# Sixty-four-row mask and shift matmuls, turned maxima, and pairwise column maxima in a two-layer transformer kernel

## What is computed

```python
h = _layernorm(x) * (1 + ca) + sa
q, k, v = heads(h @ Wq, 16), heads(h @ Wk, 4), heads(h @ Wv, 4)   # head width 64
q, k = rope(q), rope(k)                    # 4 query heads share one key head
scores = einsum('bkgqd,bkpd->bkgqp', q, k) / 8
scores = where(tril, scores, -1e30)        # query q sees keys 0..q
probs = softmax(scores)
x = x + ga * (einsum('bkgqp,bkpd->bkgqd', probs, v) @ Wo)
```

## Time and profile before

| | |
|---|---|
| median of three runs | 1842.28 us (1834.22 to 1844.19) |
| profiled execution, its own time | 1832.43 us |
| its span, first to last instruction | 1830.6 us |
| TensorE busy | 1629.2 us, 89% |
| VectorE busy | 1075.0 us, 59% |
| ScalarE busy | 703.6 us, 38% |
| mean granted TensorE clock | 0.975 of full; 1.00 in the first attention |

### The profile page before, as it was taken

The page is one execution under the profiler, slowest core; times in us unless marked ns, Lnnn a source line. Parts: engine busy times, 40 slices in busy tenths (PEclk is TensorE's granted clock), DMA queues, the critical chain, the costliest instruction groups (busy, mean ns, idle before and its releaser), DMA issues.

```text
span 1830.6 us, 75756 instructions
## 1 busy us (share of the span) xinstructions
PE 1629.2 (89%) x34444; PEld 1279.7 (70%) x34444; DVE 1075.0 (59%) x2269; ACT 703.6 (38%) x1135; POOL 847.2 (46%) x802
## 2 busy tenths in 40 slices
PE   6899999999999988888987898988989898978993
PEld 4567677777777766677975676766777677767883
DVE  3756666666688865537426566665666665544234
ACT  2334344343434333354542343433334343334341
POOL 2555555555555547437766163423324241016442
PEclk9999999999999999999987999999999999989997
DMA  9800000000000000043344433324141422036666
GB/s 302 262 18 2 8 3 8 2 8 2 8 2 2 8 4 18 15 141 41 91 70 54 86 72 68 81 47 90 43 87 46 89 59 67 15 99 187 202 205 186
DMA packets 103849, 128.05 MB, mean 70 GB/s; under 512 B 11909, under 2 KB 86281, under 8 KB 103064
## 3 DMA queue, kind: packets, MB, share of 16 engines
q1 hardware_dynamic: 82920, 103.39, 20.9%
q0 software_dynamic: 15808, 16.93, 4.9%
q10 hardware_dynamic: 4800, 2.89, 0.6%
HBM read 91.57 MB, written 54.07 MB: 80 GB/s over the span
## 4 chain that ended last, share of the span: by engine, by line
PE 60%; DVE 16%; issue 7%; POOL 6%; DMA 6%; ACT 4%; POOLq 0%; ACTq 0%; SPq 0%; DVEq 0%
PE psum L1182 57%; DVE colmax L1916 3%; DMA arena<-in_pack 3%; ACT prob L1628 2%; DVE colmax L2025 2%; DVE ctx_sum L1928 2%; DMA added_rows<-arena,slot_token 2%; POOL arena L2278 2%; DVE raw L1873 1%; DVE rowmax L1923 1%; POOL added_rows L2290 1%; PE psum L1506 1%; DVE rowmax L2033 1%; ACT arena L1645 1%; PE psum L1249 1%
## 5 line engine op out<-in xcount | busy, mean ns | idle before, releaser
L1182 PE MATMUL psum<-arena 128*32 128x32 f32 (+8 forms) x10296 | 572.6, 251 | 45.9 <-issue 24.3
L1182 PEld LDWEIGHTS psum<-arena 128*32 128x32 f32 (+3 forms) x10296 | 449.1, 126 | 135.8 <-issue 68.2
L1645 ACT ACTIVATE arena<-psum 128x1024 f32<-128x1024 f32 (+1 forms) x192 | 169.3, 882 | 310.0 <-PE psum L1182 309.9
L1182 PE MATMUL psum<-neg_ident,rowmax 128*32 128x128 bf16 (+3 forms) x4352 | 208.6, 249 | 12.9 <-DVE rowmax L2033 8.4
L1182 PE MATMUL psum<-prob,ffw 128*32 128x128 f32 x5120 | 201.5, 275 | 14.8 <-DVE rowmax L1923 13.3
L1916 DVE TENSOR_REDUCE colmax<-psum 128x512 bf16<-128x2048 f32 (+2 forms) x96 | 168.4, 1754 | 77.7 <-PE psum L1182 77.6
L2025 DVE TENSOR_REDUCE colmax<-psum 128x256 bf16<-128x768 f32 (+2 forms) x160 | 178.3, 1115 | 58.0 <-PE psum L1182 55.7
L1660 ACT COPY ctx_sum<-psum 128x384 f32<-128x384 f32 x128 | 61.2, 478 | 384.8 <-PE psum L1182 348.4
L2265 POOL TENSOR_TENSOR arena<-ctx_sum 128x256 f32<-128x256 f32 x128 | 94.2, 736 | 219.5 <-DVE ctx_sum L1928 207.9
L2033 DVE TENSOR_REDUCE rowmax<-psum 128x2 bf16<-128x256 f32 (+1 forms) x192 | 97.9, 510 | 137.2 <-PE psum L1182 136.3
L1182 PEld LDWEIGHTS psum<-neg_ident,rowmax 128*32 128x32 bf16 (+1 forms) x4352 | 135.2, 98 | 50.2 <-issue 30.6
(11 more groups left out here) (242 smaller groups left out, 2454.9 us busy)
## 6 DMA issues: line engine op xcount, KB each, us to landing
arena<-in_pack SPq DMA_DIRECT2D x39, 578.0 KB, 3.8
sent<-in_empty SPq DMA_DIRECT2D x9, 2112.0 KB, 39.9
arena<-qk_parts SPq DMA_DIRECT2D x96, 128.0 KB
q_copies<-arena SPq DMA_DIRECT2D x32, 256.0 KB
prob<-q_copies SPq DMA_DIRECT2D x128, 64.0 KB, 3.6
qk_parts<-arena SPq DMA_DIRECT2D x16, 384.0 KB, 4.9
arena<-sent SPq DMA_DIRECT2D x39, 132.0 KB, 3.2
ffw<-in_L_w SPq DMA_DIRECT2D x16, 256.0 KB, 5.7
```

The lines of the kernel that those rows point to most:

```text
L1182: return pe.matmul(o, lhsT, rhs, start=start, stop=stop, skip_group_check=True)
L1645: act.activation(probs_of(i)[:, :, h0 * P:(h0 + nh) * P], slot(n)[:, 0:(i + 1) * W].rearrange("p (j c) -> p j c", c=W), ACT.Exp, scale=HD1 ...
```

## The change

1. **Shift.** Each matmul used 128 rows and wrote 128 columns for each key block. Now it uses 64 rows (`rows`), half of them for each par: `rowmax` is laid out so that partitions 0 to 63 hold the maxima of par 0 and 64 to 127 those of par 1, with four columns x = (head a, query half). `neg_half` is minus the identity of 64, once on each half of the partitions. There are twice as many matmuls, of half the columns, and par alternates.
2. **Mask.** Four 64-row matmuls of 128 columns instead of two 128-row ones of 256: weights `later_keys` [64 queries, 128 keys] (1e30 where the key is later), `neg_half` streamed.
3. **Maxima.** To lay `rowmax` out so, the turning is done by 16 matmuls with 32 columns of `colmax` as weights, each into its own quarter of the partitions, instead of four with 128.
4. **Column maxima.** VectorE's reduction over j is replaced. ScalarE copies blocks 1 and, for i = 3, 3 to bf16 (`block_copy`); VectorE takes elementwise maxima: one for i = 1, two for i = 2, three for i = 3. The last of i = 3 has all operands in SBUF in bf16.
5. **Setup.** The `causal` constant is three times as large, and VectorE makes `neg_half` and `later_keys`.

```diff
@@ PE, scores
-                        for par in range(2):
-                            ins = mm(scores_of(u)[:, par, i, :], ident_bf[:, :],
-                                     causal[:, :].unsqueeze(1).to_broadcast([P, 2, P]), False)
+                        for half in range(2):
+                            for par in range(2):
+                                rows = slice(HQ * par, HQ * (par + 1))
+                                ins = mm(scores_of(u)[:, par, i, :].rearrange("p (a q) -> p a q", a=2)[
+                                             :, :, HQ * half:HQ * (half + 1)],
+                                         later_keys[rows, half, :],
+                                         neg_half[rows, :].unsqueeze(1).to_broadcast([HQ, 2, HQ]), False)
@@ PE, maxima
-                        for h in range(GRP):
-                            ins = mm(psum[:, CTX, h * P:(h + 1) * P], colmax[:, n % 2, h * P:(h + 1) * P],
-                                     ident_bf[:, :], start=(h == 0))
+                        for x in range(GRP):
+                            a, half = divmod(x, 2)
+                            for quad in range(GRP):
+                                par, low = divmod(quad, 2)
+                                at = (2 * par + a) * P + half * HQ + low * QUAD
+                                ins = mm(psum[QUAD * quad:QUAD * (quad + 1), CTX, x * P:(x + 1) * P],
+                                         colmax[:, n % 2, at:at + QUAD], ident_bf[:, :], start=(x == 0))
@@ PE, shift
-                        for h in range(GRP):
-                            par, a = divmod(h, 2)
+                        for x in range(GRP):
                             for j in range(0, i + 1, 2):
                                 nj = min(2, i + 1 - j)
-                                ins = mm(scores_of(u)[:, par, j:j + nj, a * P:(a + 1) * P],
-                                         rowmax[:, n % 2, h:h + 1].to_broadcast([P, P]),
-                                         neg_ident[:, :].unsqueeze(1).to_broadcast([P, nj, P]), False)
+                                for par in range(2):
+                                    rows = slice(HQ * par, HQ * (par + 1))
+                                    ins = mm(scores_of(u)[:, par, j:j + nj, x * HQ:(x + 1) * HQ],
+                                             rowmax[rows, n % 2, x:x + 1].to_broadcast([HQ, P]),
+                                             neg_half[rows, :].unsqueeze(1).to_broadcast([HQ, nj, HQ]), False)
@@ ACT
+                    elif k == "scores" and s["u"]["i"]:
+                        u = s["u"]
+                        w.wait_ge(scored, u["n"] + 1)
+                        w.wait_ge(colmax_dve, cm_at[u["n"]][1] - 1)
+                        for a, j in enumerate(range(1, u["i"] + 1, 2)):
+                            act.copy(block_copy[:, a, :, :], scores_of(u)[:, :, j, :]).then_inc(block_copied, 1)
@@ DVE, scores
-                            dve.tensor_reduce(colmax[:, n % 2, :].rearrange("p (z c) -> p z c", z=2),
-                                              scores_of(u).rearrange("p z j c -> p z c j"),
-                                              AX.X, ALU.max).then_inc(colmax_dve, 1)
+                            to = colmax[:, n % 2, :].rearrange("p (z c) -> p z c", z=2)
+                            blocks = scores_of(u)
+                            copied += (i + 1) // 2
+                            w.wait_ge(block_copied, copied)
+                            if i == 1:
+                                dve.tensor_tensor(to, blocks[:, :, 0, :], block_copy[:, 0, :, :], ALU.max
+                                                  ).then_inc(colmax_dve, 1)
+                            else:
+                                dve.tensor_tensor(pair_max, blocks[:, :, 0, :], block_copy[:, 0, :, :], ALU.max
+                                                  ).then_inc(paired, 1)
+                                if i == 3:
+                                    dve.tensor_tensor(block_copy[:, 1, :, :], blocks[:, :, 2, :], block_copy[:, 1, :, :],
+                                                      ALU.max).then_inc(paired, 1)
+                                pairs += i - 1
+                                w.wait_ge(paired, pairs)
+                                dve.tensor_tensor(to, block_copy[:, 1, :, :] if i == 3 else blocks[:, :, 2, :], pair_max,
+                                                  ALU.max).then_inc(colmax_dve, 1)
```

More of the change, by code:

```diff
@@ L31 @@
 GRP = 4
+HQ = P // 2
 E, F = 8, 512
@@ L166, in shape_constants @@
         "ident": np.eye(P, dtype=np.float32),
-        "causal": np.where(p[:, None] <= p[None, :], 0.0, NEG).astype(np.float32),
+        "causal": np.stack([np.where(p[:, None] <= p[None, :], 0.0, NEG)] + [
+            np.where(p[:, None] % HQ + HQ * half >= p[None, :], 0.0, -NEG) for half in range(2)], 1).astype(np.float32),
         "first_token": (np.arange(HALF * E)[:, None] // E * S).astype(np.float32),
@@ L235, in build @@
         prob = sb("prob", [P, 2, 4 * BANK])
-        causal_f = prob[:, 0, 0:P]
+        causal_f = prob[:, 0, 0:3 * P].rearrange("p (a c) -> p a c", a=3)
         colmax = sb("colmax", [P, 2, BANK], BF16)
@@ L340, in build @@
         xn1 = ctx_sum[:, 1, 1, :].rearrange("p (n d) -> p n d", n=NT)
+        block_copy = ctx_sum[:, 1, 0, :].bitcast(BF16).rearrange("p (a z c) -> p a z c", a=2, z=2)
+        pair_max = ctx_sum[:, 1, 1, BANK // 2:].bitcast(BF16).rearrange("p (z c) -> p z c", z=2)
+        neg_half = ctx_sum[:, 1, 1, 0:HQ // 2].bitcast(BF16)
+        later_keys = ctx_sum[:, 1, 1, HQ // 2:HQ // 2 + P].bitcast(BF16).rearrange("p (a c) -> p a c", a=2)
         small = raw[:, 1, :]
@@ L1009, in build @@
             semaphore(n) for n in ("x_full", "x_loaded", "moments_ready", "normed", "rot_a", "swapped", "key_rest"))
+        block_copied, paired = semaphore("block_copied"), semaphore("paired")
         scored, colmax_dve, colmax_act, max0_full, max0_done, shifted, prob_ready, ctx_full, ctx_drained, recip = (
@@ L1779, in tile_list @@
                                       ALU.subtract).then_inc(tiles_ready, 1)
+                copied = pairs = 0
                 dve.memset(ones_bf[:, :], 1.0)
@@ L1797, in _ @@
                         dve.tensor_scalar(neg_ident[:, :], ident[:, :], -1.0, None, ALU.mult)
+                        dve.scalar_tensor_tensor(neg_half, ident[:, 0:HQ], -1.0, ident[:, HQ:P], ALU.mult, ALU.subtract)
                     elif k == "mod_first":
@@ L1825, in _ @@
                         w.wait_ge(d_x, XREST)
-                        dve.tensor_copy(causal[:, :], causal_f).then_inc(consts_ready, 1)
+                        dve.tensor_copy(causal[:, :], causal_f[:, 0, :])
+                        dve.tensor_copy(later_keys, causal_f[:, 1:3, :]).then_inc(consts_ready, 1)
                     elif k == "stat":
```

## The result

Over twenty runs of each the changed kernel took 1844.59 us and the kernel before 1837.51 us. The ratio is 1.0039, with a 95% interval of 1.0023 to 1.0056: slower by some 7 us, where 4 us faster were forecast. The profiled execution took 1840.52 us (before 1832.43). Measured twice more beside the kernel before, the changed kernel gave 1.0061 and 1.0062.

The account below looks back on a forecast made before the run. Groups were taken as TensorE-bound mostly, plus VectorE's work between i = 3 scores and values. Groups +0.07, -0.19, -0.34, +0.02 made -0.44 a batch, -3.5 over eight; taken -4: 1828.5 profiled, 1838.5 against the median, range 1823 to 1856.

Parts of the forecast that it names:

- Leg 3: TensorE from the shift of i = 2 to the mask, 4.30 us in the second group: forecast -0.37 us.
- leg 2: From the mask after the i = 3 shift to the values, 3.79 us in the second group: forecast +0.03 us.
- leg 4: From the mask of i = 3 to the values, 4.80 us in the second group: forecast +0.51 us.
- two new changes +0.20: Tile-shape changes added on TensorE, shift to side step and side step to maxima: forecast +0.20 us in leg 1.
- leg 1: TensorE from the shift of i = 3 to the mask, 250.98 to 255.50 in the second group: forecast -0.36 us.
- the fourth group's +0.02: Forecast sum over the fourth group of a batch: leg 1 0, leg 2 -0.12, total +0.02 us.
- 1 to 2 us: Batches 5 and 6, where expert selection loads VectorE: its shorter work may give 1 to 2 us.
- theory 1: Steady groups: TensorE's 64-row shift, mask and turned maxima gain; casts and pairwise maxima lose, above all in leg 4.
- theory 2: Start of batch 0: the loss is made there, costing 7 us, and the steady state hardly moves.
- Rival 2: VectorE's detour in leg 4 decides, slower once it grows more than 0.62 us: about +11, 1853 us; chance 0.20.
- Rival 3: 64-row bf16 pairs don't run at once, +24, 1866 us, chance 0.09; in experiments, tile changes cost TensorE more than saved.
- Rival 1: The gain arrives: leg 4 keeps its 4.80 us, -2.48 a batch, -20 in all, 1822 us; chance 0.16.

Follow-up runs that it names:

- the two half kernels: Kernel before with 64-row shift, mask and turned maxima, reduction kept: 1937.69 us, ratio 0.9941; kernel before with only casts and pairwise maxima: 1968.36 us, 1.0105.
- one-cast run: Changed kernel with one block copied for i = 3 instead of two, second and third maxima reading a block from PSUM: 1944.57 us, ratio 1.0032.
- spread fills: Kernel before with routing-buffer fills moved from the start, two behind each of the first three batches' rows, one behind each of the next three: ratio 1.0004.
- the pairwise half: Kernel before with only ScalarE's casts and VectorE's pairwise maxima of the change: 1968.36 us, ratio 1.0105.
- TensorE's half alone: Changed kernel with VectorE's reduction put back and the casts left out: 1937.69 us, ratio 0.9941 against the kernel before; again 0.9969.

## Why the prediction was wrong

**Right in mechanism and size.** Leg 3 gave -0.41 (forecast -0.37), leg 2 +0.09 (+0.03) and leg 4 +0.52 (+0.51); the last maximum, taken at 0.43 from the cast, took 0.42. Pairs of 64-row bf16 matmuls run at once. A tile change behind the mask is worth what was said. The balance of a group, TensorE's saving against the longer wait behind i = 3, is what the two half kernels show.

**Mis-sized: the changes into a side step.** In the second group "two new changes +0.20" of leg 1 cost 0.31: 0.11 behind the shift, and the projection from its start to the maxima 1.98 instead of 1.78 (before, the maxima start at 253.65). Leg 1 gave -0.24 instead of -0.36 there and in the third group; in the first and fourth it gave -0.18 and -0.08, each 0.08 more than forecast. The third and fourth groups lose 0.09 and 0.06 in side steps behind the values, for which nothing was forecast. Leg 2 came out 0.17 dearer over a batch, leg 3 0.16 cheaper. Together some 0.25 a batch.

**Failed: the fourth group's +0.02.** The sum gave leg 4 the same +0.51 in all groups. It was +0.89 there: VectorE's last maximum is held by GpSimd's product, and behind it the shuffle must wait for that product anyhow. The wait is the larger of the two: without any pairwise maxima leg 4 still grew by 0.42 (5.30), and with the reduction for i = 3 by 0.76 (5.64). The one-cast run takes away the hold alone: of the 0.36 that were missed 0.13 come back, and 0.1 of that is the shorter chain, which the other groups gained too. I had named the hold among the things that would show the forecast wrong, and priced it at nothing; GpSimd's product as what the shuffle waits for was in no leg. The Trainium skill (SBUF — State Buffer, Who interferes with whom) says that a VectorE instruction with two SBUF inputs contends with a GpSimd instruction that reads SBUF, and that the second to start is blocked until the first ends. The trace agrees, ten times in 32 (every maximum that began during a product, save the four in its last 0.02 us), with an end 0.28 to 0.30 behind GpSimd's; what it cost on the critical path is less than the 5.1 us that it sums to.

These terms, of which the fourth group's leg 4 is 0.38, make +0.22 a batch of -0.44, some 5 us over eight batches.

**Failed: "the larger constant and one more VectorE copy before the first scores may cost 1."** The start of batch 0 was the steady state's sum to me. In the profiled execution it holds 6.3 of the 8.1 us. 3.4 are two stalls for instructions (2.39, and 0.99 up to 77.76 us). About 2 is the clock: unit 2's exponential starts 2.1 us late there, and on time in the second profile of the changed kernel, where the clock in 40 to 46 us was full. The fall at this place is not the change's alone: the kernel before with spread fills shows 0.83 from 36 to 46, behind 2.38 us of idling, and the pairwise half none of it behind the same 3.02 us. No run here says what decides. The stalls are the change's in the profiles, but how much of the 7 us of the medians they are stays open, since moving the fills costs elsewhere what it saves.

**Undone: "1 to 2 us" gained in expert selection.** Part of the gain is there: from unit 80 to unit 111, through batches 5 and 6, the changed kernel gets 1.0 us nearer (7.6 to 6.6 behind). Then it loses 2.4 us at one step, from unit 111 to 112, and 1.4 from 119 to 120, the two places of half clock. At the first, the same 80 matmuls take 4.81 us instead of 3.01, so 1.8 of the 2.4 is the clock's:

```profile
700.42:703.43 3.01, 3.01 (x80) 2.81 (x81) 1.33 (x2) 0.48 (x1) 1.73 (x2) 1.00 0.07 22
707.70:712.51 4.81, 4.81 (x80) 4.26 (x81) 1.02 (x2) 0.68 (x2) 1.72 (x2) 0.63 0.07 17
```

(before, then after). At the second, a held maximum of 1.41 us lies on the chain of waits just ahead of TensorE, and the clock adds to it; the two were not taken apart.

**Left out: the clock.** The prediction has no term for it. In the profiled execution the first attention holds 20.5 us of half clock, where the kernel before had none, and in the medians the mean clock is lower too, as above. An estimated 4 of the 8.1 us are the clock's by the two stretches that could be measured, 2.1 and 1.8.

Added up for the profiled execution, which was forecast 4 faster and was 8.1 slower: the groups 5.3, the start 5.1 beyond its 1, batches 5 to 7 3.0 (forecast -1.5, measured 2.2 less the groups' 0.7), 0.4 in batches 1 to 4 beyond the steady groups, and -1.7 behind the attention, 12.1 in all. So each theory has its part: theory 1 that of the groups, which the half kernels show, and theory 2 that of the start, which is there in the profiles and not settled in the medians.

Rival 2 named the place (leg 4, VectorE's detour) and the sign; its threshold of 0.62 a leg was passed in one group of four only. Rival 3 is refuted. Rival 1, the gain without the longer leg 4, is what TensorE's half alone does in the groups, -2.41 a batch where -2.48 was forecast; its time does not arrive in full: 0.994 and 0.997 for a forecast of 0.989.

## What to carry to other kernels

When a change makes one engine's work shorter and another's path longer, measure the halves alone: here a gain of 0.3 to 0.6% was bundled with a loss of 1.0%, and the better kernel is the change without its pairwise maxima. Price a chain of dependent small instructions by where its last one ends, not by busy time, and repeat the sum for every group whose neighbours differ; the group in which GpSimd was 0.04 us from being late took 0.38 of a batch's 0.66 us of error. Compare the mean granted clock of both kernels before a gain in the groups is taken for a gain in time. A VectorE instruction with two operands in SBUF is priced with what GpSimd does beside it.

## What the runs showed of the hardware

- TensorE seems to run out of instructions. Seventeen stalls of 0.9 to 4.3 us without any engine to wait for ended 1.09 to 1.59 us after a 16 KB instruction packet had landed, only while other transfers kept the DMA engines at a share near 1.0, and only in kernels with matmuls split into more and shorter ones.
- A VectorE maximum of two SBUF operands took 0.42 us alone and up to 1.41 us beside a GpSimd product, ending 0.28 to 0.30 us after it in ten cases of ten; with one operand in PSUM it took 0.69 in every case.
- A change of tile shape cost 0.10 to 0.11 us in bf16, and another 0.1 where a 128-row fp32 step followed 64-row bf16 matmuls.
- TensorE's clock fell to half at the first idle stretch of batch 0 (3.02 us) in two of three profiles of the changed kernel. In the third it stayed full there, and was half from 58.55 to 61.96 us, just behind a stall of 2.78 us.
- At half clock 80 matmuls of the values and the router took 4.81 us instead of 3.01, though only 3.6 of the 4.81 us were at half clock.
- Kernels with 64-row bf16 matmuls ran at a mean granted clock 0.0016 to 0.0063 below the kernel before, and among twenty runs of one kernel the time rose by 14 us for each 0.01 of lost clock.
